# Keeping the silu product of a state-space layer in SBUF instead of writing it back into its PSUM bank

## The chip, the cores and the metric

The kernel runs on one core of a Trainium2 chip. The metric is the device time of one execution, in microseconds; the lowest is best. Three runs of the kernel before took 918.2, 919.2 and 917.9 us, median 918.2.

Engine names are those of the profile: PE is the matrix engine (PEld its weight loads), DVE the vector engine, ACT the scalar engine, POOL the GpSimd engine, SP the engine that issues most DMAs. SBUF is the on-chip working memory, PSUM the memory of eight banks into which PE writes its products.

## The reference

The input x has shape (2, 4096, 512). Two layers follow one another, each on a layer-normalised x and added to it:

```
s    = sigmoid(silu(xn @ s_w1.T + s_b1) @ s_w2.T + s_b2)     # 512 -> 256 -> 128
u    = (xn @ B_w.T + B_b) * s
h_t  = h_{t-1} @ A.T + u_t                                   # scan over 4096 steps, 128 states
y    = h @ C_w.T + C_b + xn @ D_w.T + D_b
x1   = x + y * sigmoid(xn @ g_w.T + g_b)
e    = argmax(x1n @ gate_w.T)                                # 1 of 8 experts for each token
out  = x1 + x1n + x1n @ expert_w[e].T
```

Only the silu of the first line is touched by the change: `silu(v) = v * sigmoid(v)` with `v = xn @ s_w1.T + s_b1`.

## The kernel before

**Tiling.** The 8192 tokens are cut into 16 blocks (NBLK) of 512 tokens, b = 0 to 15. A block has its features along the 128 partitions and its tokens along the columns, so the 256 hidden units of s_w1 are two tiles of 128x512, m = 0 and m = 1 (KH = 2). A float32 product is made of three products of a high and a low part: a value is rounded to its high part (`_hi`, by a Copy into type fp32r), and the low part (`_lo`) is the value less the high part. After the 16 blocks come the experts: slots of 128 rows each, sorted by expert.

**Order.** Each engine has its own list of instructions, written out by hand, and executes it in that order; semaphores, by name in `S_`, tie the lists together. Nothing is reordered at run time. The function `body` of each engine is one block. In a block b > 0 the work of block b - 1 is finished too (its "tail": residual, second layer norm, scores, places in the lists).

**The silu part of a block.** The names and lines are those that the prediction uses.
- PE (L1640, L1644) computes tile m into PSUM bank TP ("turned", m = 0) or G ("gates", m = 1).
- ACT L802 writes sigmoid(bank + b1) into `silu[:, m, :]`, in SBUF.
- DVE L1189 (`silu_product`) multiplies (bank + b1) by `silu`, and writes the product back into the PSUM bank.
- ACT L809 copies the bank to `sT[0]` (siluT_hi).
- DVE L1184 (`silu_lo`) writes bank less `sT[0]` to `sT[1]` (siluT_lo).
- PE waits for `silu_lo` of both tiles, and then makes the six products of s_w2 into bank SC ("scores", L1454 to L1456), of which ACT L820 makes `select`, and DVE L1198 (`u_in_pairs`) u, named z. L1021 and L1023 split z into z_half_hi and z_half_lo, with which PE starts the scan (`to_pairs`).

Between the end of tile m = 1 and the six products of s_w2, PE has 21 products of 128x512 columns: twelve for B_w and nine for D_w (`y_dense(b, 0, 0, 1, 2)`). The scan goes on in steps (`to_chunks`, `over`, L1599) which PE and DVE take in turn, with dense products of D_w and g_w in PE's list between them.

**Beside it.** In the same stretch POOL works through `residual(b - 1)`: four pairs of 128x512 operations on SBUF, L586 (y times gate) and L589 (add to x). Then come `rstd1` (L572 to L579), `scatter` (L611, four indirect DMAs) and `add_identity` (L620). DVE has, between and behind its silu operations, layer-norm statistics and `low_piece` (L1220), a difference of two 128x512 tiles in SBUF. `low_piece` stands in DVE's list ahead of `u_in_pairs`.

The operations of `silu`, once per tile m, before the change:

Of the kernel before, what the change touches and what calls it, by code (L numbers as in the profile page):

```python
# [5 lines left out]
def preln_ssm_moe_kernel(nc, x, A, B_w, B_b, C_w, C_b, D_w, D_b, s_w1, s_b1, s_w2, s_b2, g_w, g_b,  # L6
# [14 lines left out]
    f32, f32r, bf16 = mybir.dt.float32, mybir.dt.float32r, mybir.dt.bfloat16  # L21
    i32, u16 = mybir.dt.int32, mybir.dt.uint16
    ALU, ACT, AX = mybir.AluOpType, mybir.ActivationFunctionType, mybir.AxisListType
# [45 lines left out]
    def wait(eng, sem, value):  # L69

        if not isinstance(value, int) or value > 0:
            eng.wait_ge(sem, value)

    with ExitStack() as keep:
        def psum(name):
            return keep.enter_context(nc.psum_tensor(name, [P, 512], f32))
# [8 lines left out]
        G, TP, SA, SC = psum("gates"), psum("turned"), psum("scan"), psum("scores")  # L85
# [51 lines left out]
        with ExitStack() as main:  # L137
            def sb(name, shape, dt=f32):
                return main.enter_context(nc.sbuf_tensor(name, shape, dt))

            def pair(name, shape):
                return sb(name + "_hi", shape, f32r), sb(name + "_lo", shape, f32r)
# [9 lines left out]
            silu = sb("silu", [P, KH, TB])  # L152

            sT, s2T = pair("siluT", [P, KH, TB]), pair("s2T", [P, KH, NS])
# [12 lines left out]
            b1, b2, bB = sb("s_b1_col", [P, KH]), sb("s_b2_col", [P, 1]), sb("B_b_col", [P, 1])  # L167
# [15 lines left out]
        S_ = {}  # L183
# [32 lines left out]
        def by_block(bank):  # L216
            return bank[:].rearrange("p (k t) -> p k t", k=KD)
# [6 lines left out]
        def in_pairs(t, cols=CW):  # L224

            return t[:, 0:cols].rearrange("p (c n) -> p c n", n=NB)
# [85 lines left out]
        def by_dma(b, i):  # L312

            return 0 < b < LASTB - 1 and i >= NT // 2
# [362 lines left out]
        def _(act):  # L677
# [5 lines left out]
            def prep(stage):  # L683

                for what, n in STAGES[stage]:
                    if what == "pow":
                        act.wait_ge(S_["pow_psum"], n + 1)
                        for i, (side, k, _, _) in enumerate(ROUNDS[n]):
                            nc.scalar.activation(tslot(k) if side == "T" else pslot(k),
                                                 POW_BANK[:, i * NS:(i + 1) * NS], ACT.Copy  # L690
                                                 ).then_inc(S_["pow_copied"], 1)
                    else:
                        act.wait_ge(S_["w_turned"], n + 1)
                        nc.scalar.activation(JOBS[n][2][0], job_view(n), ACT.Copy).then_inc(S_["w_hi"], 1)
# [55 lines left out]
            def halve_piece(b, j):  # L750

                act.wait_ge(w_ident[j], b + 1)
                wait(act, w_flip[j], 16 * b)
                nc.scalar.activation(w_halves[j].rearrange("p (h d) -> p h d", h=2), planes(w_raw[j]), ACT.Copy
                                     ).then_inc(w_halved[j], 1)
# [22 lines left out]
            def high(b, i):  # L778
                act.wait_ge(S_["joined"], turn_of(b, i) + 1)
                act.wait_ge(S_["g_psum"], NT * (b - 1) + i + 1)  # L780
                nc.scalar.activation(xT[0][:, :, i * P:(i + 1) * P], joined[turn_of(b, i) % 2][:], ACT.Copy
                                     ).then_inc(S_["xT_hi"], 1)

            def body(b):
                tail = b > 0
                ahead = b < LASTB
                dma = by_dma(b - 1, NT - 1)
                if tail:
                    high(b, NT - 1)
                    if b > 1:  # L790
                        halve_piece(b, 0)
                else:
                    for i in range(NT):
                        act.wait_ge(S_["xT_psum"], i + 1)

                        nc.scalar.activation(xT[0][:, :, i * P:(i + 1) * P], by_block(XT_BANKS[i]), ACT.Copy
                                             ).then_inc(S_["xT_hi"], 1)
                    prep(1)
                for m in range(KH):
                    act.wait_ge(S_["s1_psum"], KH * b + m + 1)  # L800
                    wait(act, S_["silu_lo"], KH * (b - 1) + m + 1)
                    nc.scalar.activation(silu[:, m, :], (TP, G)[m][:], ACT.Sigmoid, bias=b1[:, m:m + 1]  # L802
                                         ).then_inc(S_["s1_sig"], 1)
                    if tail and m == 0:
                        gates(b - 1, NT - 1)
                    if not tail:
                        prep(2 + m)
                    act.wait_ge(S_["silu_ready"], KH * b + m + 1)
                    nc.scalar.activation(sT[0][:, m, :], (TP, G)[m][:], ACT.Copy).then_inc(S_["silu_hi"], 1)  # L809
                if b == 1:  # L810
                    join_piece(0, 0)
                if tail:
                    join_piece(b - 1, 1)
                    if b > 1:
                        halve_piece(b, 1)
                else:
                    prep(2 + KH)
                    powers_hi()
                act.wait_ge(S_["s2_psum"], b + 1)
                nc.scalar.activation(sel[:], SC[:], ACT.Sigmoid, bias=b2[:]).then_inc(S_["sel_ready"], 1)  # L820
                if tail:
                    tail_hi(b - 1, 0)
                    tail_hi(b - 1, 1)
                if b == 1:
                    halve_piece(1, 0)
                    halve_piece(1, 1)
                if dma:
                    halve_x1(b - 1, 2)
                    halve_x1(b - 1, 3)
                if ahead:  # L830
                    halve(b + 1, 0)
                    halve(b + 1, 1)
                else:
                    join_piece(b, 0)
                    join_piece(b, 1)
                if tail and not dma:
                    tail_hi(b - 1, 2)
                    tail_hi(b - 1, 3)
                if tail:
                    scoresT(b - 1, 0)  # L840
                if dma:
                    for i in range(2, NT):
                        join_x1(b - 1, i)
                        tail_hi(b - 1, i)
                if tail and ahead:
                    join_piece(b, 0)
                if ahead:
                    join(b + 1, 0)
                gates(b, 0)
                if ahead:  # L850
                    high(b + 1, 0)
                    halve(b + 1, 2)
                    join(b + 1, 1)
                if dma:
                    gates(b, 1)
                if tail:
                    scoresT(b - 1, 1)
                if not dma:
                    gates(b, 1)
                if ahead:  # L860
                    high(b + 1, 1)
                    halve(b + 1, 3)
                    if not dma:
                        join(b + 1, 2)
                act.wait_ge(S_["scan_lo"], NSTEP * (b + 1))
                for half, h in zip(zp, hT):
                    ins = nc.scalar.activation(h[:, :, J - 1, :], in_pairs(half), ACT.Copy)
                ins.then_inc(S_["h_last"], 1)
                gates(b, 2)
                act.wait_ge(S_["h_sum"], b + 1)  # L870
                nc.scalar.activation(hT[0][:, :, 0, :], first_of, ACT.Copy).then_inc(S_["h_hi"], 1)
                if ahead:
                    if dma:
                        join(b + 1, 2)
                    high(b + 1, 2)
                    join(b + 1, 3)
                if not tail:
                    halve_piece(0, 0)
                    halve_piece(0, 1)
# [85 lines left out]
        def _(dve):  # L965
# [215 lines left out]

            def silu_lo(b, m):
                dve.wait_ge(S_["silu_hi"], KH * b + m + 1)
                nc.vector.tensor_tensor(sT[1][:, m, :], (TP, G)[m][:], sT[0][:, m, :].bitcast(f32),  # L1184
                                        ALU.subtract).then_inc(S_["silu_lo"], 1)

            def silu_product(b, m):
                dve.wait_ge(S_["s1_sig"], KH * b + m + 1)
                nc.vector.scalar_tensor_tensor((TP, G)[m][:], (TP, G)[m][:], b1[:, m:m + 1], silu[:, m, :],  # L1189
                                               ALU.add, ALU.mult).then_inc(S_["silu_ready"], 1)  # L1190

            def u_in_pairs(b):
# [636 lines left out]
```

## Time and profile before

| | us |
|---|---|
| median of three runs | 918.2 |
| the profiled execution | 918.2 |
| its span | 916.5 |
| PE busy in it | 895.1 |
| DVE busy | 678.7 |
| ACT busy | 652.4 |
| POOL busy | 385.0 |

The span is the time from the first to the last instruction that the profile shows. An engine's busy time counts the time in which it executes at least one instruction, without waits. The granted clock of PE has a mean of 0.997 of full speed. Blocks 3 to 14 last about 41 us each in the trace.

### The profile page before, as it was taken

What the parts mean: (1) busy time and instruction counts of PE and PEld (TensorE: products, weight loads), DVE (VectorE), ACT (ScalarE), POOL (GpSimd) and SP (SyncE); (2) the same over time, 40 slices, a digit from 0 to 9 for tenths busy, and PEclk for the clock granted to TensorE, in tenths of its full rate; (3) what the DMA queues carried; (4) which work ended last, traced back from release to release, by engine and by line L of the source; (5) the groups of instructions that cost most, each with busy time, mean ns of one, the idle gap of its engine ahead of it and who ended that gap; (6) DMA issues with size and microseconds to landing.
All of it is one profiled execution on the core that took longest, in us unless ns stands there. A gap on an engine that the chain in (4) does not pass through costs nothing.

```text
span 916.5 us, 15673 instructions
## 1 busy us (share of the span) xinstructions
PE 895.1 (98%) x4461; PEld 722.6 (79%) x4462; DVE 678.7 (74%) x1697; ACT 652.4 (71%) x878; POOL 385.0 (42%) x520
## 2 busy tenths in 40 slices
PE   8999999999999999999999999999999999999995
PEld 7777878787878878787878878787878887888884
DVE  6778878788887878788887878787786465555552
ACT  5578697978878797978878797978534446666661
POOL 1032536181634527181634527172423453443432
PEclk9999999999999999999999999999999999999998
DMA  8435395867778485868768485877889879898871
GB/s 312 134 92 142 89 219 129 191 161 186 144 169 202 103 213 137 200 154 182 160 148 207 106 207 150 198 146 176 297 266 418 317 246 255 213 222 209 199 186 38
DMA packets 231048, 172.35 MB, mean 188 GB/s; under 512 B 155701, under 2 KB 189237, under 8 KB 229952
## 3 DMA queue, kind: packets, MB, share of 16 engines
q1 hardware_dynamic: 220032, 137.71, 61.0%
q0 software_dynamic: 10800, 33.70, 11.3%
q8 instruction: 35, 0.57, 0.3%
q14 instruction: 37, 0.30, 0.1%
q10 hardware_dynamic: 144, 0.07, 0.0%
HBM read 81.63 MB, written 54.68 MB: 149 GB/s over the span
## 4 chain that ended last, share of the span: by engine, by line
PE 91%; DVE 2%; issue 1%; DMA 1%; SPq 1%; ACT 1%; POOL 0%; DVEq 0%; POOLq 0%; ACTq 0%
PE y L1756 22%; PE y L1454 8%; PE y L1456 8%; PE y L1455 8%; PE gates L1454 7%; PE gates L1456 6%; PE gates L1455 6%; PE scan L1599 4%; PE turned L1640 3%; PE gates L1640 3%; PE scan L1454 2%; PE scan L1456 2%; PE scan L1455 2%; PE turned L1744 2%; PE turned L1644 1%; PE gates L1644 1%
## 5 line engine op out<-in xcount | busy, mean ns | idle before, releaser
L1756 PE MATMUL y<-experts,x1T_hi 128*128 x568 | 180.7, 399 | 3.0 <-issue 2.1
L595 POOL TENSOR_SCALAR ln_var_eps<-ln_mean_var 128x4 f32<-128x4 f32 x16 | 3.6, 224 | 294.1 <-DVE ln_mean_var L1076 294.0
L1756 PEld LDWEIGHTS y<-experts,x1T_hi 128*128 128x128 f32 x568 | 103.3, 188 | 24.4 <-issue 4.7
L650 POOL DMA_INDIRECT out<-gate,ids x71 | 72.6, 1022 | 116.2 <-DVE gate L1419 79.2
L1756 PE MATMUL y<-experts,x1T_lo 128*128 x284 | 111.4, 392 | 0.0
L1454 PE MATMUL gates<-GwT_hi,xT_hi 128*128 128x512 f32 x256 | 104.0, 406 | 0.0
L1454 PE MATMUL y<-DwT_hi,xT_hi 128*128 128x512 f32 x256 | 102.6, 401 | 0.5 <-DVE gateT L998 0.5
L1419 DVE TENSOR_TENSOR gate<-y,raw_weights 128x512 f32<-128x512 f32 x71 | 49.1, 691 | 71.7 <-PE y L1756 69.2
L1456 PE MATMUL gates<-GwT_hi,xT_lo 128*128 128x512 f32 x256 | 100.4, 392 | 0.0
L1455 PE MATMUL gates<-GwT_lo,xT_hi 128*128 128x512 f32 x256 | 100.2, 391 | 0.0
L1456 PE MATMUL y<-DwT_hi,xT_lo 128*128 128x512 f32 x256 | 100.1, 391 | 0.0
L1455 PE MATMUL y<-DwT_lo,xT_hi 128*128 128x512 f32 x256 | 100.1, 391 | 0.0
L774 ACT ACTIVATE joined<-flipped 128x1024 uint16<-128x1024 uint16 x60 | 82.1, 1368 | 10.0 <-DMA flipped<-halves 7.6
L586 POOL TENSOR_TENSOR y_biased<-y_biased,gate 128x512 f32<-128x512 f32 x60 | 78.0, 1301 | 25.5 <-DVE y_biased L1066 25.5
L589 POOL TENSOR_TENSOR x_rows<-x_rows,y_biased 128x512 f32<-128x512 f32 x60 | 82.4, 1373 | 4.7
L611 POOL DMA_INDIRECT routed_rows<-x_rows,dest x64 | 63.9, 999 | 23.4 <-issue 22.5
L888 ACT ACTIVATE x1T_hi<-turned 128x512 fp32r<-128x512 f32 x36 | 21.6, 599 | 70.2 <-PE turned L1744 70.2
L1029 DVE TENSOR_TENSOR z<-scan,z 128x126 f32<-128x126 f32 (+6 forms) x128 | 35.7, 279 | 43.2 <-PE scan L1599 41.6
L747 ACT ACTIVATE halves<-x_in 128x1024 uint16<-128x1024 uint16 x60 | 63.4, 1057 | 1.9
L1756 PEld LDWEIGHTS y<-experts,x1T_lo 128*128 128x128 f32 x284 | 53.3, 188 | 11.9
L1456 PEld LDWEIGHTS gates<-GwT_hi,xT_lo 128*128 128x128 f32 x256 | 48.0, 188 | 11.2
L1456 PEld LDWEIGHTS y<-DwT_hi,xT_lo 128*128 128x128 f32 x256 | 48.0, 188 | 10.5
(283 smaller groups left out, 2333.1 us busy)
## 6 DMA issues: line engine op xcount, KB each, us to landing
raw_weights<-routed_rows SPq DMA_DIRECT2D x71, 258.0 KB, 3.2
x_in<-L_attn_x SPq DMA_DIRECT2D x32, 512.0 KB, 4.3
x_rows<-L_attn_x SPq DMA_DIRECT2D x32, 512.0 KB, 5.1
turned_experts<-raw_weights SPq DMA_DIRECT2D x32, 512.0 KB, 4.1
experts<-turned_experts SPq DMA_DIRECT2D x8, 2048.0 KB, 14.4
raw_weights<-L_ffn_expert_w SPq DMA_DIRECT2D x32, 256.0 KB, 2.9
routed_rows<-padrow SPq DMA_DIRECT2D x9, 258.0 KB, 4.2
out<-gate,ids POOLq DMA_INDIRECT x71, 4.1
```

Of the source, the lines that this page charges most:

```text
L586: nc.gpsimd.tensor_tensor(yb[:, i, :], yb[:, i, :], gate[:, i, :], ALU.mult).then_inc(S_["gated"], 1)
L589: nc.gpsimd.tensor_tensor(xrow[q][:, i, 0:D], xrow[q][:, i, 0:D], yb[:, i, :], ALU.add).then_inc(S_["x1_ready"], 1)
L611: nc.gpsimd.indirect_dma_start(out=routed, out_offset=bass.IndirectOffsetOnAxis(ap=dest[q][:, i:i + 1], axis=0), in_=xrow[q][:, i, :], in_ ...
L650: nc.gpsimd.indirect_dma_start(out=out_rows, out_offset=bass.IndirectOffsetOnAxis(ap=ids[r][:, 0:1], axis=0), in_=res[r], in_offset=None, ...
L747: nc.scalar.activation(halves[n % 2][:].rearrange("p (h d) -> p h d", h=2), planes(xin[:, i, :]), ACT.Copy).then_inc(S_["x_halves"], 1)
L774: nc.scalar.activation(planes(joined[n % 2][:].rearrange("p k t -> p (k t)")), flipped[n % 2][:].rearrange("p (h k) t -> p h (k t)", h=2), ...
L1419: nc.vector.tensor_tensor(res[r], Y[m % 2][:], rows[m][:, 0:D], ALU.add).then_inc(S_["slot_result"], 1)
L1454: nc.tensor.matmul(dst, left[0], right[0], start=first, stop=False)
L1455: nc.tensor.matmul(dst, left[0], right[1], start=False, stop=False)
L1456: return nc.tensor.matmul(dst, left[1], right[0], start=False, stop=last)
L1640: nc.tensor.matmul((TP, G)[m][:], h[:, k, m * P:(m + 1) * P], xT[0][:, k, :], start=(k == 0 and h is s1T[0]), stop=False)
L1756: ins = nc.tensor.matmul(Y[m % 2][:], x2T[a][:, k, m % 2 * P:(m % 2 + 1) * P], flat[:, bass.ds(first + (w * KD + k) * D, D)], start=(k == ...
```

## The change

The product of DVE L1189 goes to `silu[:, m, :]` in SBUF, over the sigmoid that it reads, and no longer to the PSUM bank. ACT L809 and DVE L1184 read it from there. No instruction is added or taken away, and every wait and signal is as it was.

```diff
@@ scalar engine, body(b)
                     act.wait_ge(S_["silu_ready"], KH * b + m + 1)
-                    nc.scalar.activation(sT[0][:, m, :], (TP, G)[m][:], ACT.Copy).then_inc(S_["silu_hi"], 1)
+                    nc.scalar.activation(sT[0][:, m, :], silu[:, m, :], ACT.Copy).then_inc(S_["silu_hi"], 1)
@@ vector engine
             def silu_lo(b, m):
                 dve.wait_ge(S_["silu_hi"], KH * b + m + 1)
-                nc.vector.tensor_tensor(sT[1][:, m, :], (TP, G)[m][:], sT[0][:, m, :].bitcast(f32),
+                nc.vector.tensor_tensor(sT[1][:, m, :], silu[:, m, :], sT[0][:, m, :].bitcast(f32),
                                         ALU.subtract).then_inc(S_["silu_lo"], 1)
 
             def silu_product(b, m):
                 dve.wait_ge(S_["s1_sig"], KH * b + m + 1)
-                nc.vector.scalar_tensor_tensor((TP, G)[m][:], (TP, G)[m][:], b1[:, m:m + 1], silu[:, m, :],
+                nc.vector.scalar_tensor_tensor(silu[:, m, :], (TP, G)[m][:], b1[:, m:m + 1], silu[:, m, :],
                                                ALU.add, ALU.mult).then_inc(S_["silu_ready"], 1)
```

ACT's next sigmoid into `silu[:, m, :]` (block b + 1) waits, in both kernels, for `silu_lo` of block b.

## Rows read from the trace of the kernel before

**Rows 1.** The page's first part: busy us, share of the span, instructions.
```profile
PE 895.1 (98%) x4461; PEld 722.6 (79%) x4462; DVE 678.7 (74%) x1697; ACT 652.4 (71%) x878; POOL 385.0 (42%) x520
```

**Rows 2.** Waits of PE: engine, line, releaser: us in total, times, longest.
```profile
PE scan L1454 <- DVE z_half_lo L1023: 1.5, 3, 0.7
```

**Rows 3.** Timeline of DVE, block 8: start us, us, what, [idle before <-releaser].
```profile
354.41 0.69 DVE L1184 TENSOR_TENSOR siluT_lo<-turned,siluT_hi 128x512 fp32r<-128x512 f32 x1
355.57 0.76 DVE L1189 SCALAR_TENSOR_TENSOR gates<-gates,s_b_col,silu 128x512 f32<-128x512 f32 x1 [0.47 <-ACT silu L802]
357.00 0.69 DVE L1184 TENSOR_TENSOR siluT_lo<-gates,siluT_hi 128x512 fp32r<-128x512 f32 x1
359.08 1.06 DVE L1220 TENSOR_TENSOR raw_weights<-raw_weights 128x512 fp32r<-128x512 f32 x1
361.69 0.87 DVE L1198 SCALAR_TENSOR_TENSOR z<-scan,B_b_col,select 128x256 f32<-128x256 f32 x2 [1.56 <-ACT select L820]
363.12 0.43 DVE L1023 TENSOR_TENSOR z_half_lo<-z,z_half_hi 128x256 fp32r<-128x256 f32 x1
```

**Rows 4.** Timeline of POOL, block 8.
```profile
354.40 1.30 POOL L589 TENSOR_TENSOR x_rows<-x_rows,y_biased 128x512 f32<-128x512 f32 x1
357.03 1.30 POOL L589 TENSOR_TENSOR x_rows<-x_rows,y_biased 128x512 f32<-128x512 f32 x1
358.29 1.30 POOL L586 TENSOR_TENSOR y_biased<-y_biased,gate 128x512 f32<-128x512 f32 x1
359.67 1.62 POOL L589 TENSOR_TENSOR x_rows<-x_rows,y_biased 128x512 f32<-128x512 f32 x1
...
368.09 0.97 POOL L611 DMA_INDIRECT routed_rows<-x_rows,dest  x1 [0.30 <-issue]
```

**Rows 5.** Timeline of ACT, block 8.
```profile
348.14 0.63 ACT L781 ACTIVATE xT_hi<-joined 128x512 fp32r<-128x512 f32 x1
356.37 0.60 ACT L809 ACTIVATE siluT_hi<-gates 128x512 fp32r<-128x512 f32 x1 [0.82 <-DVE gates L1189]
360.97 0.69 ACT L820 ACTIVATE select<-scores,s_b_col 128x512 f32<-128x512 f32 x1 [1.11 <-PE scores L1456]
```

**Rows 6.** Timeline of PE's weight loads, block 8.
```profile
359.19 0.19 PEld L1454 LDWEIGHTS scores<-siluT_hi,s2T_hi 128*128 128x128 f32 x1
363.60 0.19 PEld L1454 LDWEIGHTS scan<-z_half_hi,A_powers_hi 128*128 128x128 f32 x1 [0.15 <-DVE z_half_lo L1023]
370.18 0.19 PEld L1599 LDWEIGHTS scan<-chunk_ends,A_powers_hi 128*128 128x128 f32 x1
```

**Rows 7.** Timelines of DVE and POOL, blocks 3 and 13.
```profile
149.19 0.69 DVE L1184 TENSOR_TENSOR siluT_lo<-turned,siluT_hi 128x512 fp32r<-128x512 f32 x1
149.20 1.29 POOL L589 TENSOR_TENSOR x_rows<-x_rows,y_biased 128x512 f32<-128x512 f32 x1
...
559.55 1.29 POOL L589 TENSOR_TENSOR x_rows<-x_rows,y_biased 128x512 f32<-128x512 f32 x1
559.58 0.69 DVE L1184 TENSOR_TENSOR siluT_lo<-turned,siluT_hi 128x512 fp32r<-128x512 f32 x1
```

**Rows 8.** Timelines of DVE and POOL, blocks 1 and 10.
```profile
74.18 0.37 POOL L577 TENSOR_SCALAR ln_minus_mean<-ln_mean_var 128x4 f32<-128x4 f32 x1
74.22 0.30 DVE L1021 CAST z_half_hi<-z 128x256 fp32r<-128x256 f32 x1
...
451.40 0.89 POOL L620 TENSOR_TENSOR raw_weights<-raw_weights,ident 128x128 f32<-128x128 f32 x2
451.53 0.44 DVE L1021 CAST chunk_ends<-z 128x126 fp32r<-128x126 f32 x1
```

**Rows 9.** Timelines of POOL, DVE and PE, block 2.
```profile
122.34 0.96 POOL L611 DMA_INDIRECT routed_rows<-x_rows,dest  x1 [0.30 <-issue]
122.71 0.62 DVE L1021 CAST chunk_ends<-z 128x126 fp32r<-128x126 f32 x1
...
124.02 0.38 PE L1599 MATMUL scan<-chunk_ends,A_powers_hi 128*128 128x248 f32 x1 [0.16 <-DVE chunk_ends L1023]
```

## The prediction

> **What bounds the kernel now.** I read four views. The page's first part gives PE 895.1 us of the 916.5 us span [rows 1]: the kernel is as long as PE's list. So an edit on ACT and DVE moves the time only where PE then waits. The list of PE's waits has nearly nothing from the blocks: no row for siluT_lo, and 1.5 us in all, three times, for z_half_lo, the value with which the scan starts [rows 2]. The third view is the timeline of block 8, engine by engine [rows 3 to 6]; it stands for blocks 3 to 14, which repeat it to within a few hundredths where I use it. The fourth is a search for moments at which DVE and POOL start or overlap closely [rows 7 to 9].
>
> What is to be seen in block 8: the second siluT_lo runs 357.00 to 357.69 [rows 3], and the weight load that needs it starts at 359.19 with no wait shown [rows 6]: 1.50 us of slack. Behind it DVE does statistics and L1220, which ends at 359.08 + 1.06 = 360.14; then it is idle until ACT's select ends at 360.97 + 0.69 = 361.66 [rows 5], and z starts at 361.69 [rows 3]. So L1220 has 1.5 us of slack too. Behind z there is none: z_half_lo ends at 363.12 + 0.43 = 363.55, and the weight load starts at 363.60 [rows 3, 6]. Whatever delays z delays PE one for one.
>
> **The parts of the change.** There are three instructions per tile, two tiles a block, 16 blocks.
>
> *The product L1189.* It takes 0.76 us with PSUM as its output [rows 3]. With SBUF as output the trace has none of this size; the nearest row is L1184, 0.69 from PSUM and SBUF into SBUF, another operation. So between -0.07 and 0; I take 0, since L1189 also has a bias column and a second operation, which can as well be what it costs more.
>
> *The copy L809.* 0.60 from PSUM; L781, the same copy between two SBUF tiles, took 0.63 [rows 5]. So +0.03 us, twice in the chain of a block. It is hidden by the 1.50 us. (The Trainium skill, "VectorE: DVE Perf Modes", section on the trn2 errata, gives ScalarE a fixed 224 cycles from SBUF against 172 from PSUM. That would be +0.04 by its figures, an estimate; the trace's rows say 0.03, and the sum is the same by either.)
>
> *The difference L1184.* This is the part that matters. It now reads PSUM and SBUF; it will read two SBUF tiles, as L1220 does. L1220 has the same shape and took 1.06 us, not 0.69. POOL's L586 ran 358.29 to 359.59, across its start; L1220 ended 0.55 after that, at 360.14; and POOL's next operation, started at 359.67, took 1.62 for the usual 1.30 and ended 1.15 after L1220 [rows 3, 4]. So the two wait for each other: DVE's operation ends 0.55 after the POOL operation in its way, and the POOL operation behind ends 0.55 + 1.15 = 1.70 after the one before it, 0.32 more than usual. L1184 of today is free of this: at 357.00 it ran 0.69 beside POOL's 357.03 [rows 3, 4].
>
> The Trainium skill, "SBUF — State Buffer", section "SBUF: two separate sides", states it as a rule: a VectorE operation with two SBUF inputs and a GpSimd operation that reads SBUF exclude one another for the whole instruction, and whichever starts first goes first. It speaks against this change, and L1220's row agrees with it.
>
> POOL is busy without a pause while both L1184 run, so both must meet it. I follow block 8 through.
>
> First L1184: it starts 0.01 after POOL's L589 (354.41 and 354.40); over blocks 3 to 14, twelve of them, the lag is between -0.01 and +0.03 [rows 7], and becomes -0.04 to +0.06 with the product's and the copy's terms. Who goes first? A cast of DVE that started 0.04 after a POOL operation took 0.30 for 256 columns, so went first; one that started 0.13 after took 0.44 for 126 columns, so did not [rows 8]. The border lies between 0.04 and 0.13; most of my lags lie below, and I take DVE first. Then this L1184 ends at 354.44 + 0.69 = 355.13, in time for the second product, which waits for ACT until 355.57 [rows 3]. POOL's L589 ends at 355.13 + 1.15 = 356.28 instead of 355.70.
>
> Second L1184: ready at 357.06. POOL's L586 runs 356.24 to 357.54 by then; L1184 ends at 357.54 + 0.55 = 358.09, 0.40 late. PE needs it at 359.19: 1.1 us of slack left. Cost nothing.
>
> POOL behind it: L589 ends at 357.54 + 1.70 = 359.24, L586 at 360.50. L1220 is ready at 359.47 and meets this L586: it ends at 360.50 + 0.55 = 361.05. z cannot start before 361.69: still 0.6 us of slack, cost nothing. POOL's last L589 ends at 360.50 + 1.70 = 362.20 instead of 361.29, so everything behind it on POOL's queue (rstd1, the scatter's four DMAs, L620) comes 0.9 us later. ACT's next normalisation waits for rstd1: 0 if ACT comes to it later anyway, 0.9 us a block at most if not; I take 0, because ACT is busy for 71% of the span [rows 1] and its delay has still to reach PE. The scatter's rows are not needed for many blocks.
>
> Sum for blocks 3 to 14: 0. Block 0 has no POOL work beside it. Blocks 1, 2 and 15 meet POOL at other phases; I allow 0.3 us for them together, from block 1, where POOL leads clearly and the slack is about used up. Against the profiled execution's 918.2 us, which is also the median of the runs: 918.5 us.
>
> **The rivals.**
>
> *POOL goes first (slower).* The place is the first L1184; the price follows from the border in rows 8: if POOL gets there first, this L1184 waits for L589's end at 355.70 and ends at 356.25. The second product starts at 356.17, the second L1184 is ready at 357.61 and meets L589, now until 358.78: it ends at 359.33, PE loads 0.2 late. L1220 is ready at 360.72 and waits until 361.86: end 362.41; z starts at 362.33 instead of 361.69. PE loses 0.6 us in a block: 12 x 0.6 = 7 us, 925.5. If POOL's next L586, which starts right behind L589 with no gap, keeps DVE out once more, L1184 ends 1.3 us later still, the second at 360.47, and PE loses 359.19 to 360.52: 12 x 1.3 = 16 us, 934. For it: the lag is a few hundredths, on a clock of which I know POOL's starts roughly. Against it: the cast of rows 8 that went first at 0.04. It decides from a lag between 0.04 and 0.13.
>
> *POOL's lateness breaks a later scan step (slower).* In block 2 a scatter DMA started 0.37 before a cast of the scan: the cast took 0.62, and PE's scan product came late, with 0.16 us idle shown [rows 9]. In block 8 the step's weight load stands at 370.18, hardly behind its value. The scatter's fourth DMA, at 368.09 [rows 4], will be at 369.0, and that cast, less than a microsecond ahead of the load at 370.18, falls right into it. If this repeats, 0.16 to 0.4 us a block: 2 to 5 us, 920 to 923. The same holds, smaller, for z's own split, which has no slack.
>
> *The change does not do this.* If two SBUF inputs cost nothing here, everything but the 0.03 of the copy stays: 918.2. L1220's row speaks against it.
>
> *A gain.* The product 0.07 shorter, or PE's 1.5 us for z_half_lo gone [rows 2], which would need z earlier; but z waits for select, and select for PE. At most 1.5 us: 916.7. I find no path to it.
>
> **How the numbers follow.** Two runs of this kernel differ by up to 1.3 us, so I call within 0.2%, 1.8 us, no change. The forecast has a chance of 0.55. POOL first: 0.21 (925.5 with 0.15, 934 with 0.06). The later scan step, or POOL first in some blocks only: 0.15, 920 to 923. No effect at all: 0.06. A gain: 0.03. So same 0.61, slower 0.36, faster 0.03. The range runs from 917.0 to 926.5: it holds the forecast, no effect, the scan step, and the cheaper form of POOL first; it leaves out the dearer form and the edges.
>
> **What would show it.** In the trace after: the second L1184 at about 1.0 us instead of 0.69, the first at 0.69 (forecast) or about 1.8 (POOL first); POOL's fourth operation at about 1.9 instead of 1.30; L1220 at about 1.6, ending before z starts; L809 at 0.63; L1189 at 0.69 to 0.76. No row of PE waiting for siluT_lo, and the wait for z_half_lo as before. The prediction is wrong if the period of a block grows, or if L1184 stays at 0.69 in all blocks, or if L1220 ends behind select.

## The result and the profile after

The changed kernel took 926.95 us (median of 4 runs, 926.61 to 933.0) against 918.27 us: a ratio of 1.011, 95% interval 1.0076 to 1.0144, slower. (The ratios of this document are taken over all runs of both kernels; the quotient of these two medians alone is 1.0095.) On a second chip, where the kernel before took 920.4 us, the same kernel (e9 below) had 1.0074 (1.0048 to 1.0100); the two intervals overlap. The profiled execution took 927.61 us, span 925.9 us, 9.4 us more than before.

The page of the changed kernel: its first part, which answers to [rows 1], and the waits of PE, which answer to [rows 2].

```profile
PE 901.9 (97%) x4461; PEld 722.7 (78%) x4462; DVE 713.1 (77%) x1697; ACT 653.0 (71%) x878; POOL 399.7 (43%) x520
```
```profile
PE scan L1454 <- DVE z_half_lo L1023: 5.2, 15, 1.3
PE scan L1599 <- DVE chunk_ends L1023: 2.7, 8, 0.8
```

DVE has the same 1697 instructions and is busy for 34.4 us more, POOL for 14.7 us more. So operations have become longer, not more. PE waited for z_half_lo three times in the kernel before, and does so 15 times now: at the same three places, and once more in each of blocks 3 to 14, for 0.20 to 0.26 us each.

**The silu part of block 8.** The timelines of DVE, POOL, ACT and PE's weight loads in the changed kernel, as in [rows 3 to 6]. Everything in this block stands about 4 us later than before.

```profile
358.53 1.80 DVE L1184 TENSOR_TENSOR siluT_lo<-silu,siluT_hi 128x512 fp32r<-128x512 f32 x1
360.25 0.74 DVE L1189 SCALAR_TENSOR_TENSOR silu<-gates,s_b_col,silu 128x512 f32<-128x512 f32 x1
361.69 1.72 DVE L1184 TENSOR_TENSOR siluT_lo<-silu,siluT_hi 128x512 fp32r<-128x512 f32 x1
364.81 1.67 DVE L1220 TENSOR_TENSOR raw_weights<-raw_weights 128x512 fp32r<-128x512 f32 x1
366.40 0.86 DVE L1198 SCALAR_TENSOR_TENSOR z<-scan,B_b_col,select 128x256 f32<-128x256 f32 x2
```
```profile
358.48 1.30 POOL L589 TENSOR_TENSOR x_rows<-x_rows,y_biased 128x512 f32<-128x512 f32 x1
359.74 1.74 POOL L586 TENSOR_TENSOR y_biased<-y_biased,gate 128x512 f32<-128x512 f32 x1
361.56 1.30 POOL L589 TENSOR_TENSOR x_rows<-x_rows,y_biased 128x512 f32<-128x512 f32 x1
362.81 1.75 POOL L586 TENSOR_TENSOR y_biased<-y_biased,gate 128x512 f32<-128x512 f32 x1
364.64 1.29 POOL L589 TENSOR_TENSOR x_rows<-x_rows,y_biased 128x512 f32<-128x512 f32 x1
```
```profile
361.02 0.64 ACT L809 ACTIVATE siluT_hi<-silu 128x512 fp32r<-128x512 f32 x1 [1.40 <-DVE silu L1189]
365.15 0.69 ACT L820 ACTIVATE select<-scores,s_b_col 128x512 f32<-128x512 f32 x1 [0.61 <-PE scores L1456]
```
```profile
363.46 0.19 PEld L1454 LDWEIGHTS scores<-siluT_hi,s2T_hi 128*128 128x128 f32 x1 [0.23 <-DVE siluT_lo L1184]
368.30 0.19 PEld L1454 LDWEIGHTS scan<-z_half_hi,A_powers_hi 128*128 128x128 f32 x1 [0.67 <-DVE z_half_lo L1023]
```

What is to be seen: the first L1184 started 0.05 us after POOL's L589 and took 1.80 us instead of 0.69. It ended at 360.33, which is L589's end, 359.78, and 0.55. The second L1184 met the next L589 and took 1.72; L1220 met the last one and took 1.67. Each ended 0.55 after the POOL operation in its way, and the two L586 behind the two L1184 took 1.74 and 1.75. L1220 ended at 366.48, later than select (365.84), so z no longer waits for ACT: it starts at 366.40, behind L1220. This is the rival "POOL goes first" of the prediction, in its cheaper form.

**Where PE lost the time.** Both kernels give PE the same products in the same order. For each product I took its start in the one trace less its start in the other; where this difference grows, PE lost time. Summed by place over all blocks, in us, against the profiled execution of the kernel before:

| kernel | six products of s_w2 | scan's start, z | step over, l = 1 | scan steps behind it | all else | whole |
|---|---|---|---|---|---|---|
| changed | 1.4 | 7.0 | 3.4 | -0.2 | -2.1 | 9.4 |
| changed again (e9) | 1.7 | 7.0 | 2.0 | -0.1 | -1.8 | 8.8 |
| e1 difference from PSUM | 0.0 | 0.1 | 0.5 | 0.2 | 2.2 | 2.9 |
| e2 difference alone | 1.7 | 7.0 | 2.8 | -0.1 | -1.8 | 9.6 |
| e3 short residual | 0.0 | -0.7 | -0.6 | 1.0 | 6.1 | 5.7 |
| e4 POOL later | 0.4 | 1.6 | 3.3 | 0.4 | 0.2 | 5.8 |
| e5 statistic later | 2.7 | 0.5 | 2.2 | -0.4 | 1.8 | 6.8 |
| e6 identity first | 1.5 | 7.0 | -0.6 | 4.3 | 0.3 | 12.5 |
| e8 POOL later, identity first | 0.4 | 1.0 | -0.6 | 4.2 | -0.7 | 4.3 |
| e10 POOL later, short identity | 0.0 | 1.2 | -0.6 | 1.6 | -1.1 | 1.2 |
| e11 short identity | 1.6 | 6.9 | 1.3 | -0.2 | 1.8 | 11.3 |
| e7 before, identity first | 0.0 | 0.2 | -0.6 | 1.0 | -2.5 | -1.8 |

The step over, l = 1, is the PE product whose weights were loaded at 370.18 in [rows 6]; "scan steps behind it" counts the dense products beside these steps too. In the column of over, l = 1, the value -0.6 means that nothing is lost there: 0.4 of it is what the kernel before itself lost in block 2 [rows 9].

"All else" holds the differences between one execution or chip and the next as well (the first loads, the expert slots): only the four named columns repeat well enough to read. Median times and ratios, below, are the measure of the whole.

**The step over, l = 1**, in block 8. In the kernel before, the fourth scatter DMA of [rows 4] had ended, at 369.06, when DVE's cast for this step started:

```profile
369.31 0.34 DVE L1021 CAST chunk_ends<-z 128x126 fp32r<-128x126 f32 x1
```

In the changed kernel, POOL, DVE and PE's weight load:

```profile
373.24 0.96 POOL L611 DMA_INDIRECT routed_rows<-x_rows,dest  x1 [0.30 <-issue]
374.23 0.89 POOL L620 TENSOR_TENSOR raw_weights<-raw_weights,ident 128x128 f32<-128x128 f32 x2
374.01 0.78 DVE L1021 CAST chunk_ends<-z 128x126 fp32r<-128x126 f32 x1
374.83 0.44 DVE L1023 TENSOR_TENSOR chunk_ends<-z,chunk_ends 128x126 fp32r<-128x126 f32 x1
375.32 0.19 PEld L1599 LDWEIGHTS scan<-chunk_ends,A_powers_hi 128*128 128x128 f32 x1 [0.59 <-DVE chunk_ends L1023]
```

POOL now comes to the end of its scatter at just this step. The cast took 0.78 and the weight load came late. Whether the DMA or the two L620 behind it (one row here) are to blame, this view doesn't tell; e10 does.

Not all of the 3.4 us is of this kind. 1.1 us of it comes from block 7 alone, where both parts of the split ran at full speed and DVE's first operation of the step was late. PE's product before it had ended at 330.63:

```profile
332.04 0.29 DVE L1029 TENSOR_TENSOR z<-scan,z 128x126 f32<-128x126 f32 x1 [2.23 <-PE scan L1599]
```

In blocks 1 to 14 of the kernel before, L1029 started 0.04 us after the end of its product at every step. What held it for 1.37 us more here the profile does not show.

### The profile page after: what moved, and what is told of

Read it like the earlier page. It is cut to its first block, busy times and chain, and to the rows that moved or that the text cites. A ratio compares the mean times of both kernels' runs of the same rounds, so it can differ in the third digit from the quotient of the medians.

```text
span 925.9 us, 15673 instructions
## 1 busy us (share of the span) xinstructions
PE 901.9 (97%) x4461; PEld 722.7 (78%) x4462; DVE 713.1 (77%) x1697; ACT 653.0 (71%) x878; POOL 399.7 (43%) x520
## 4 chain that ended last, share of the span: by engine, by line
PE 69%; DVE 19%; issue 5%; ACT 2%; POOL 0%; DVEq 0%; ACTq 0%; POOLq 0%
PE y L1756 21%; PE gates L1454 6%; PE gates L1456 6%; PE gates L1455 6%; PE y L1454 6%; PE y L1456 5%; PE y L1455 5%; PE scan L1599 4%; DVE y_biased L1066 3%; DVE siluT_lo L1184 3%; DVE silu L1189 2%; DVE ln_stats L971 2%; ACT siluT_hi L809 2%; PE turned L1744 2%; DVE ln_stats L1070 1%
## 5 line engine op out<-in xcount | busy, mean ns | idle before, releaser
L586 POOL TENSOR_TENSOR y_biased<-y_biased,gate 128x512 f32<-128x512 f32 x60 | 90.1, 1502 | 25.5 <-DVE y_biased L1066 25.5
L589 POOL TENSOR_TENSOR x_rows<-x_rows,y_biased 128x512 f32<-128x512 f32 x60 | 79.6, 1327 | 4.7
L1029 DVE TENSOR_TENSOR z<-scan,z 128x126 f32<-128x126 f32 (+6 forms) x128 | 35.8, 280 | 44.2 <-PE scan L1599 34.5
L1456 PEld LDWEIGHTS gates<-GwT_hi,xT_lo 128*128 128x128 f32 x256 | 48.0, 188 | 11.3
```

Of the source, the lines that this page charges most:

```text
L586: nc.gpsimd.tensor_tensor(yb[:, i, :], yb[:, i, :], gate[:, i, :], ALU.mult).then_inc(S_["gated"], 1)
L589: nc.gpsimd.tensor_tensor(xrow[q][:, i, 0:D], xrow[q][:, i, 0:D], yb[:, i, :], ALU.add).then_inc(S_["x1_ready"], 1)
L1456: return nc.tensor.matmul(dst, left[1], right[0], start=False, stop=last)
```

## Experiments

All runs are compared with the kernel before on their own chip (920.6 us for e1 to e4, 920.4 for e5, e6, e8 and e9, 919.9 for e7, e10 and e11). The times in the expectations suppose 918.3 for it, so the ratio is what they are to be held against.

**e1: only the difference reads PSUM again**

```diff
-                nc.vector.tensor_tensor(sT[1][:, m, :], silu[:, m, :], sT[0][:, m, :].bitcast(f32),
+                nc.vector.tensor_tensor(sT[1][:, m, :], (TP, G)[m][:], sT[0][:, m, :].bitcast(f32),
```


> The changed kernel, but the difference L1184 takes the PSUM bank again as its first operand, with siluT_hi from SBUF as its second. Leaves out: the low part is then bank less siluT_hi, where the bank holds the sum before the silu, so siluT_lo is not the reference's. Product to SBUF and copy from SBUF stay. Theory 1 (two SBUF inputs shut DVE and POOL out of each other, and POOL wins the start of the first L1184): both L1184 back at 0.69 us, POOL's eight operations at 1.30 except the last, time 918 to 919 us. Rival 2 (the slower copy and the product's new output alone shift DVE enough to upset the block): still 924 us or more.

Measured: ratio 1.0005 (0.9990 to 1.0019). DVE and POOL in block 8 of e1:

```profile
355.22 0.69 DVE L1184 TENSOR_TENSOR siluT_lo<-turned,siluT_hi 128x512 fp32r<-128x512 f32 x1
357.79 0.69 DVE L1184 TENSOR_TENSOR siluT_lo<-gates,siluT_hi 128x512 fp32r<-128x512 f32 x1
359.87 1.05 DVE L1220 TENSOR_TENSOR raw_weights<-raw_weights 128x512 fp32r<-128x512 f32 x1
```
```profile
355.18 1.30 POOL L589 TENSOR_TENSOR x_rows<-x_rows,y_biased 128x512 f32<-128x512 f32 x1
357.81 1.31 POOL L589 TENSOR_TENSOR x_rows<-x_rows,y_biased 128x512 f32<-128x512 f32 x1
```

The first L1184 stands 0.04 behind L589, as in the changed kernel, and is not held. So the whole loss hangs on L1184's first operand. The product's new output and the slower copy cost nothing.

**e2: the difference alone**

```diff
 (kernel before)
-                nc.vector.tensor_tensor(sT[1][:, m, :], (TP, G)[m][:], sT[0][:, m, :].bitcast(f32),
+                nc.vector.tensor_tensor(sT[1][:, m, :], silu[:, m, :], sT[0][:, m, :].bitcast(f32),
```


> The kernel before, but the difference L1184 takes silu in SBUF as its first operand. Leaves out: silu holds the sigmoid there, so siluT_lo is not the reference's. Product and copy stay in PSUM, so the first L1184 becomes ready about 0.03 us earlier than in the changed kernel. Theory 1: L1184 meets POOL as in the changed kernel. If the border between who goes first lies below a lag of 0.01 us, all blocks lose as in the changed kernel, 925 to 927 us; if it lies between 0.02 and 0.05, DVE goes first (first L1184 0.69 us) and the time is 918 to 920 us. Rival 2: 918.3 us with L1184 at 0.69 in all places.

Measured: ratio 1.0084 (1.0067 to 1.0101), 927.89 us; the table's columns are those of the changed kernel. In e2 the lags of blocks 3 to 14 lie at 0.01 to 0.04, and POOL won all twelve. Block 6, with the smallest lag, shows it (POOL and DVE in e2):

```profile
274.61 1.29 POOL L589 TENSOR_TENSOR x_rows<-x_rows,y_biased 128x512 f32<-128x512 f32 x1
274.62 1.82 DVE L1184 TENSOR_TENSOR siluT_lo<-silu,siluT_hi 128x512 fp32r<-128x512 f32 x1
```

So the copy's 0.03 us did not decide it: a lag of 0.01 is enough to lose.

**e3: a short residual**

```diff
-                    nc.gpsimd.tensor_tensor(yb[:, i, :], yb[:, i, :], gate[:, i, :], ALU.mult
+                    nc.gpsimd.tensor_tensor(yb[:, i, 0:16], yb[:, i, 0:16], gate[:, i, 0:16], ALU.mult
...
-                    nc.gpsimd.tensor_tensor(xrow[q][:, i, 0:D], xrow[q][:, i, 0:D], yb[:, i, :],
+                    nc.gpsimd.tensor_tensor(xrow[q][:, i, 0:16], xrow[q][:, i, 0:16], yb[:, i, 0:16],
```


> The changed kernel, with POOL's residual L586 and L589 on 16 of 512 columns. Leaves out: the rest of y times gate is not added to x, so the output is not the reference's. Theory 1: POOL is out of the way when L1184 runs; L1184 and L1220 take 0.69, no stall of PE for z_half_lo, 917.5 to 919 us. Rival 2 (operands alone): 925 us or more.

Measured: ratio 1.0063 (1.0046 to 1.0080): a miss. What was said of the instructions came out (L1184 0.69 in blocks 1 to 15, L1220 0.66 to 0.69, no growth at the scan's start), but POOL now comes to its scatter and to L620 some 2 us earlier against DVE, and these meet another scan step. In block 8 of e3 (POOL, DVE, PE's weight load):

```profile
371.39 0.90 POOL L620 TENSOR_TENSOR raw_weights<-raw_weights,ident 128x128 f32<-128x128 f32 x2
371.45 0.52 DVE L1021 CAST chunk_ends<-z 128x128 fp32r<-128x128 f32 x1
372.00 0.45 DVE L1023 TENSOR_TENSOR chunk_ends<-z,chunk_ends 128x128 fp32r<-128x128 f32 x1
372.50 0.19 PEld L1599 LDWEIGHTS scan<-chunk_ends,A_powers_hi 128*128 128x128 f32 x1 [0.34 <-DVE chunk_ends L1023]
```

That step is over, l = 0; it makes 2.6 us of e3's "all else". The rest, among it 3.0 us at the head of the blocks, I have not traced. The run is no test of the first L1184; it shows that whatever moves POOL against DVE can cost half a per cent.

**e4: POOL a little later**

```diff
                     pool.wait_ge(S_["yb_ready"], NT * b + i + 1)
+                    if i == 0:
+                        nc.gpsimd.memset(spacer[:], 0.0)
```


> The changed kernel, with one small memset (128x16) of POOL ahead of the first operation of each residual, so POOL's eight operations start some 0.1 to 0.2 us later. Theory 1: in blocks 3 to 14 DVE now starts the first L1184 ahead of POOL; it takes 0.69, the second about 1.0 to 1.2, POOL's fourth operation about 1.9, L1220 ends before select, and PE's wait for z_half_lo goes; 919 to 922 us (the scan step behind the scatter may still be late). Rival 3 (it is not who starts first, any meeting costs the block the same): 926 to 928 us. Rival 2: 927 us.

Measured: 924.34 us, ratio 1.0045 (1.0029 to 1.0062); on a kernel before of 918.3 that is 922.4, just beyond the expected 922; the rest as theory 1 has it. The memset moved POOL by only some 0.05 us, enough in blocks 3 to 13, not in 14. (In block 12 the first L1184 came some 0.3 us ahead of POOL's L589, was held a little by the L586 before it, and took 0.76.) Blocks 4 and 14 of e4; the line numbers of e4, e8 and e10 are 3 higher from here on, so L1187 is L1184 and L592 is L589:

```profile
190.62 0.69 DVE L1187 TENSOR_TENSOR siluT_lo<-silu,siluT_hi 128x512 fp32r<-128x512 f32 x1
190.62 1.85 POOL L592 TENSOR_TENSOR x_rows<-x_rows,y_biased 128x512 f32<-128x512 f32 x1
193.21 1.08 DVE L1187 TENSOR_TENSOR siluT_lo<-silu,siluT_hi 128x512 fp32r<-128x512 f32 x1
...
604.90 1.29 POOL L592 TENSOR_TENSOR x_rows<-x_rows,y_biased 128x512 f32<-128x512 f32 x1
604.92 1.83 DVE L1187 TENSOR_TENSOR siluT_lo<-silu,siluT_hi 128x512 fp32r<-128x512 f32 x1
```

At a lag of 0.00 DVE went first, at 0.02 POOL did. With DVE first the block runs as the prediction had it: 0.69, then 1.08, POOL's fourth operation 1.85. The column of the scan's start falls from 7.0 to 1.6 us. The step over, l = 1, stays at 3.3: it is a loss of its own, which comes with POOL's lateness, whoever goes first.

**e5: one statistic of DVE moved out of the way of L1220**

```diff
                 if tail:
                     ln2_stats(old, oldq, 0)
-                    ln2_stats(old, oldq, 1)
...
                 to_chunks(b)
+                if tail:
+                    ln2_stats(old, oldq, 1)
```


> The changed kernel, with one layer-norm statistic of DVE (ln2_stats of tile 1, 0.6 us) moved from ahead of L1220 to behind the scan step to_chunks, where DVE is idle. Theory 1 splits the loss into about 7 us at the scan's start (z late behind L1220) and 3.4 us at the scan step behind the scatter (over, l = 1). L1220 then meets an earlier operation of POOL and ends before select: the 7 us at the scan's start go, the 3.4 us stay; ratio to the kernel before 1.003 to 1.006. Rival 4 (the lateness comes down through ACT or the second L1184, not through L1220): ratio still 1.009 to 1.012.

Measured: ratio 1.0051 (1.0038 to 1.0065), as expected; the scan's start falls from 7.0 to 0.5 us though both L1184 still take 1.7 to 1.8. DVE in block 8 of e5:

```profile
360.00 1.73 DVE L1184 TENSOR_TENSOR siluT_lo<-silu,siluT_hi 128x512 fp32r<-128x512 f32 x1
362.53 0.91 DVE L1220 TENSOR_TENSOR raw_weights<-raw_weights 128x512 fp32r<-128x512 f32 x1
364.20 0.88 DVE L1198 SCALAR_TENSOR_TENSOR z<-scan,B_b_col,select 128x256 f32<-128x256 f32 x2 [0.76 <-ACT select L820]
```

z waits for select again. So the 7 us came down through L1220, the operation between the second L1184 and z.

**e6: L620 ahead of the scatter**

```diff
+                if 0 < b < LASTB:
+                    for j in range(2):
+                        add_identity(b + 1, j)
                 if b >= 2:
                     scatter(b - 2, q)
-                if 0 < b < LASTB:
-                    for j in range(2):
-                        add_identity(b + 1, j)
```


> The changed kernel, with POOL's two add_identity operations L620 ahead of the four scatter DMAs L611 instead of behind them. Theory 1, second part (POOL's lateness puts L620 beside the casts of the scan step over, l = 1): that step's lateness of 3.4 us falls to under 1 us, the 7 us at the scan's start stay; ratio 1.006 to 1.009. Rival 5 (the scatter DMAs themselves, not L620, keep the cast out): the step stays late by 2 us or more, ratio 1.009 to 1.013.

Measured: ratio 1.0081 (1.0059 to 1.0103), no gain over the changed kernel. The step over, l = 1, went from 2.0 (e9) or 3.4 to -0.6 us, and the cast is not held although a scatter DMA lies across it: in block 8 of e6 the DMA runs from 374.12 to 375.08, and the cast started at 374.36 and took 0.24. That rules out rival 5. But 4.3 us appeared at the next step and the dense products beside it. There, in block 8 of e6, neither the cast nor the difference is slowed; the step's first DVE operation starts late:

```profile
375.46 0.28 PE L1599 MATMUL scan<-chunk_ends,A_powers_lo 128*128 128x248 f32 x1
376.37 0.30 DVE L1029 TENSOR_TENSOR z<-scan,z 128x124 f32<-128x124 f32 x1 [0.84 <-PE scan L1599]
377.64 0.19 PEld L1599 LDWEIGHTS scan<-chunk_ends,A_powers_hi 128*128 128x128 f32 x1 [0.25 <-DVE chunk_ends L1023]
```

PE's product ended at 375.74, and DVE had been idle since 375.54. What held its L1029 until 376.37, 0.63 instead of 0.04 after the product, the profile does not show, and it stays open. POOL does nothing at that time.

**e8: both, POOL later and L620 first** (the memset of e4 with 128 columns, and the edit of e6)

> The changed kernel, with POOL's residual put off by a memset of 128x128, so that DVE starts the first L1184 clearly ahead of it in blocks 3 to 14, and L620 ahead of the scatter as well. Theory 1, both parts: nothing is left of the loss but block 1; ratio 0.999 to 1.003. If only the meeting at the first L1184 matters: the same as e4, 1.004 to 1.005.

Measured: ratio 1.0015 (0.9992 to 1.0038). The first L1184 took 0.69 us in eleven of the blocks 3 to 14 and 0.88 in one; scan's start 1.0 us, over -0.6. Left is the 4.2 us of e6's late step. The time of the changed kernel is nearly all back.

**e9: the changed kernel again**

> The changed kernel itself, on the chip of the three others of this group. Every theory: ratio 1.009 to 1.012, first L1184 1.8 us in blocks 3 to 14.

Measured: 927.58 us, ratio 1.0074 (1.0048 to 1.0100), a little under the 1.009 expected; first L1184 1.8 us in the blocks read. Its 7.0 us at the scan's start repeat; the step over, l = 1, is the part that varies from execution to execution (2.0 and 3.4), mostly by the late L1029 of block 7, which e9 does not have.

**e10: POOL later, and a short L620 in its old place**

```diff
-                part = w_raw[j][:, f * P:(f + 1) * P]
-                nc.gpsimd.tensor_tensor(part, part, ident[:], ALU.add).then_inc(w_ident[j], 1)
+                part = w_raw[j][:, f * P:f * P + 4]
+                nc.gpsimd.tensor_tensor(part, part, ident[:, 0:4], ALU.add).then_inc(w_ident[j], 1)
```


> The changed kernel, with POOL's residual put off by a memset of 128x128 (as in e8), and L620 in its old place on 4 of 128 columns. Leaves out: most of the identity that POOL adds to the expert weights, so the output is not the reference's. If L620 beside a cast is the second part of the loss, nothing but block 1 is left, about 1 us: ratio 0.999 to 1.002. If the scatter DMAs are it, over or the step behind it stays late by 2 us or more: 1.003 to 1.005.

Measured: ratio 0.9988 (0.9977 to 1.0000). With DVE first and no long L620 the changed kernel is as fast as the one before, its L1184 still reading two SBUF tiles. Block 4 of e10, POOL and DVE:

```profile
204.32 0.96 POOL L614 DMA_INDIRECT routed_rows<-x_rows,dest  x1 [0.30 <-issue]
204.70 0.25 DVE L1024 CAST chunk_ends<-z 128x126 fp32r<-128x126 f32 x1
```

The fourth DMA starts 0.38 us ahead of the cast, where it stands in [rows 9] (0.37) and in block 4 of e4 (0.38). There the cast took 0.62 and 0.61, with full L620 behind the DMA; here it took 0.25. So the DMA alone does not hold the cast: the long L620 has to follow. How it matters to a cast that ends just as L620's recorded start comes the traces do not show.

The account closes: of the 1.2 us left at the scan's start, block 1 has 1.0. The 1.6 us behind l = 1 are e6's late step again, in fewer blocks.

**e11: the short L620 alone** (the edit of e10 without the memset)

> The changed kernel, with L620 on 4 of 128 columns. Leaves out: most of the identity that POOL adds to the expert weights. The 7 us at the scan's start stay, the 2 to 3.4 us at over, l = 1, fall to under 1 if L620 is their cause; ratio 1.006 to 1.009. If the scatter DMAs are the cause, as the changed kernel, 1.009 or more, with that step still late.

Measured: ratio 1.0057 (1.0036 to 1.0078). The scan's start keeps 6.9 us. Over, l = 1, has 1.3 us, of which a single block, 4, brings 1.8, by an L1029 that started 2.16 us late, again with nothing in the profile that held it; the lateness in every other block or so is gone. Together with e10: the two parts are independent.

**e7: the kernel before with L620 first** (the edit of e6)

> The kernel before the change, with L620 ahead of the scatter. In it L620 slows a cast and a difference of the step over, l = 1, in each block by 0.26 us together, just hidden. Theory: the slowed step moves to the next one, as it did in e6, and the time is the same or up to 3 us more: ratio 0.999 to 1.003.

Measured: 917.28 us against 919.92, ratio 0.9970 (0.9956 to 0.9985): faster than both kernels, against my expectation. Its trace, held against the kernel before, shows 0.6 us less at over, l = 1, 1.0 us more behind it, and the rest in "all else". The two executions are of different chips, so I can't say from them where the 2.6 us come from.

## Why the prediction was wrong

*PE is the bound, an edit on DVE counts only where PE waits.* Right, and with it the sites: the two columns that grew are the two at which the prediction named no or hardly any slack.

*The product L1189 and the copy L809.* Right: 0.74 and 0.63 to 0.64 us; no cost by e1.

*Two SBUF inputs shut DVE and POOL out of each other; 0.55 and 1.70.* Right to 0.01 or 0.02 us in every place of block 8. The rule of the Trainium skill ("SBUF — State Buffer", "SBUF: two separate sides") holds here in both directions: e1 shows it from the one side, e4's 0.00 and e2's 0.01 show that the first to start goes first.

*Who goes first at the first L1184: DVE.* Wrong, and the step that failed. I read a border between 0.04 and 0.13 us from [rows 8]. For this pair it lies between 0.00 (e4) and 0.01 (e2); the changed kernel's blocks 3 to 14 came to a lag of 0.03 to 0.06 and all lost. Block 15, with DVE 0.08 ahead, won. Most of the lags that I had worked out, -0.04 to +0.06, had POOL ahead, so the forecast needed a border above them. The row that misled me is another pair: a cast with one input, and a POOL operation on 4 columns. Why it was not held is open; no experiment took that cast apart. The step rested on a few hundredths of a microsecond, in twelve blocks that are copies of each other: one coin for all twelve, and the chances were those of a coin. I gave POOL first 0.21.

*The price of POOL first.* The mechanism, PE 0.2 late at the weights, L1220 behind select, 0.6 a block, 7 us: measured 1.4 + 7.0 us, which is 0.6 in each of blocks 3 to 14, as priced, and 1.0 in block 1. POOL's next operation did not keep DVE out once more: DVE got in between two POOL operations every time, so the dearer form never came.

*POOL's lateness breaks a later scan step.* Right in the step and the size, 2.0 to 3.4 us against 2 to 5. Wrong in the instruction: I read the cast of [rows 9] as held by the scatter DMA, but with the DMA in the same place and a short L620 (e10) it took 0.25. L620, which I had only as one more thing that comes later, is what it hangs on. And wrong in its place among the cases, the second step that failed: I made it a rival to the others. It comes on top of either (e4: DVE first and 3.3 us), since POOL is late in both: from its fourth operation to the fourth DMA it takes 13.7 us in the kernel before, 14.8 in the changed kernel, 14.5 in e4 (medians of blocks 3 to 14). That is why 926.95 lies above the range's 926.5, and, for the most part, why the forecast itself, with DVE first, was some 4 us too low: e4, which runs as forecast in blocks 3 to 13, had a ratio of 1.0045 where 918.5 against 918.2 is 1.0003.

*Blocks 1, 2 and 15: 0.3 us.* Mis-sized: block 1 alone has 1.0 us of e10's scan start. In block 1 DVE does the add_identity itself (L1215) between L1184 and z, and in the kernel before its L1220 ended at 73.20 and z started at 73.13, without a wait: z had no slack there, which I had not looked up.

*ACT's normalisation behind rstd1: 0.* Right; no wait of PE for xT appears among the changed kernel's.

## What to carry to other kernels

In these traces, moving an operand from PSUM to SBUF did not make the vector operation longer by itself (L1184 0.69 us either way when POOL was out of its way), but it put it into a queue with GpSimd: with one PSUM input L1184 ran beside POOL's additions (e1), with two SBUF inputs it waited for them, or they for it. Before such a move, look what GpSimd does at that moment, and follow both lists to the next place without slack; the operation that pays may be a third one (here L1220, then z). Where a forecast hangs on which of two engines starts a hundredth earlier, it is one coin for all repetitions of the loop, and both outcomes belong into the range, with whatever both of them cause added to each.

## What the runs showed that was not expected

- DVE's operation got in between two POOL operations that followed each other without a gap (e.g. POOL's 358.48 + 1.30 and 359.74): in every such place here the waiting engine was served next, even where the recorded start of the other's next instruction was already past.
- A shift of POOL by about 0.05 us, one small memset, was worth some 3 us of 925: 1.0045 (e4) against 1.0084 on one chip (e2, whose columns are those of the changed kernel, which itself did not run there).
- The order of POOL's list costs time even though POOL is busy for only 42% of the span: L620 ahead of the scatter took 0.3% off the kernel before. Where the 2.6 us were is open.
- DVE's L1029 starts 0.04 us after its product in most places, but 0.2 to 2.2 us later in some (block 7 of the changed kernel, blocks of e6, e7, e8, e10 and e11), with DVE idle before it. Whether it is one cause the traces do not show.
